# Two transformer blocks on one Trainium2 core: head norms squared before the rotation, and a new written order of work

## The reference

```
# A: cross attention            xn = layernorm(x); yn = layernorm(ctx)
q = xn @ Wq; k, v = split(yn @ Wkv); x = x + softmax(q k^T / 4) v @ Wproj + bproj
# B: MLP                        x = x + gelu(layernorm(x) @ W1 + b1) @ W2 + b2      (256 -> 1024 -> 256)
# C: cross attention with rotated, normalised heads
xn = x * rsqrt(mean(x*x) + 1e-5) * norm_w
q, k, v = xn @ wq, ctx @ wkv
q, k = rotate(q), rotate(k)     # x * cos + concat(-x2, x1) * sin in each head
q = q / max(norm(q), 1e-12); k = k / max(norm(k), 1e-12)     # per head
x = x + softmax(4 * q k^T) v @ wout
```

## Time and profile before

| | us |
|---|---|
| time, median of 3 runs | 364.57 |
| time of the profiled execution | 364.86 |
| its span, first to last instruction | 363.0 |
| TensorE busy | 350.7 |
| VectorE busy | 273.1 |
| ScalarE busy | 263.8 |
| GpSimd busy | 192.9 |

### The profile page before, as it was taken

How to read it: one execution, slowest core, us unless ns; L and a number is a source line. 1 busy time by engine, 2 the same in 40 slices (tenths; PEclk the granted TensorE clock), 3 DMA queues, 4 the chain that set the end, 5 groups by cost and what they waited for, 6 DMA issues and landing times.

```text
span 363.0 us, 11434 instructions
## 1 busy us (share of the span) xinstructions
PE 350.7 (97%) x4497; PEld 318.6 (88%) x4497; DVE 273.1 (75%) x654; ACT 263.8 (73%) x533; POOL 192.9 (53%) x194
## 2 busy tenths in 40 slices
PE   7799899999999999999999999999999999999996
PEld 7688788878878889999999999998989999988885
DVE  4869978988977985758578787687877756868742
ACT  3575676769677578849497896977988959975662
POOL 2553480875734261121974679637839476295910
PEclk9999999999999999999999999999999999999999
DMA  7940602001001000010001000001001010100000
GB/s 220 293 128 3 205 2 61 32 3 32 2 2 31 5 2 3 2 31 2 0 17 32 16 2 3 13 29 45 20 2 43 2 47 31 31 16 16 17 31 30
DMA packets 14837, 13.60 MB, mean 37 GB/s; under 512 B 1473, under 2 KB 14017, under 8 KB 14785
## 3 DMA queue, kind: packets, MB, share of 16 engines
q1 hardware_dynamic: 14640, 12.87, 11.5%
q10 hardware_dynamic: 144, 0.01, 0.0%
HBM read 10.78 MB, written 2.10 MB: 35 GB/s over the span
## 4 chain that ended last, share of the span: by engine, by line
PE 51%; POOL 5%; issue 2%; DVE 2%; ACT 2%; POOLq 2%; ACTq 0%; DVEq 0%
PE banks_s L1257 11%; PE bank_o L1269 7%; PE bank_y L1269 6%; PE bank_qk L1096 5%; POOL norm_inv L403 4%; PE bank_y L1323 3%; PE banks_s L1312 3%; PE bank_qk L1102 2%; PE bank_t L1102 2%; POOLq L65 1%; PE bank_o L1303 1%; PE bank_y L1330 1%; PE bank_t L1210 1%; PE bank_y L1096 1%; PE banks_s L1175 1%
## 5 line engine op out<-in xcount | busy, mean ns | idle before, releaser
L403 POOL TENSOR_TENSOR norm_inv<-norm_sq_min,minus_half 128x32 f32<-128x32 f32 x16 | 88.0, 5502 | 25.7 <-DVE norm_sq_min L2388 25.7
L357 POOL TENSOR_TENSOR masked<-qkT_r,cols 128x512 fp32r<-128x512 f32 x32 | 32.6, 1039 | 40.8 <-issue 21.9
L2296 DVE TENSOR_REDUCE row_max<-banks_s 128x8 f32<-128x1024 f32 x32 | 37.6, 1217 | 2.4 <-PE banks_s L1175 2.2
L617 ACT ACTIVATE PT<-banks_s 128x1024 f32<-128x1024 f32 x32 | 31.1, 1023 | 6.2 <-PE banks_s L1199 6.1
L1257 PE MATMUL banks_s<-lnT_hi,W_hi 128*128 128x256 f32 x120 | 35.4, 295 | 0.0
L717 ACT ACTIVATE PT<-banks_s 128x1024 f32<-128x1024 f32 x32 | 31.5, 1022 | 4.6 <-PE banks_s L1312 4.6
L1257 PE MATMUL banks_s<-lnT_hi,W_lo 128*128 128x256 f32 x120 | 33.9, 282 | 0.0
L1257 PE MATMUL banks_s<-lnT_lo,W_hi 128*128 128x256 f32 x120 | 33.8, 282 | 0.0
L1175 PE MATMUL banks_s<-masked,qkT_r 32*128 32x256 f32 x768 | 31.5, 293 | 2.2 <-DVE row_max L2296 1.0
L1175 PEld LDWEIGHTS banks_s<-masked,qkT_r 32*128 32x128 f32 x768 | 25.0, 183 | 8.2 <-issue 3.5
L396 POOL TENSOR_TENSOR cT_r<-ctx_in,cT_r 128x256 fp32r<-128x256 f32 x16 | 11.7, 738 | 36.7 <-ACT cT_r L687 36.7
(11 more groups left out here) (193 smaller groups left out, 1074.8 us busy)
## 6 DMA issues: line engine op xcount, KB each, us to landing
x_all<-in_x SPq DMA_DIRECT2D x16, 128.0 KB, 3.3
ctx_in<-in_ctx SPq DMA_DIRECT2D x16, 128.0 KB, 4.5
W_s<-in_L_xattn_W SPq DMA_DIRECT2D x2, 1024.0 KB, 8.3
ctx_in<-in_ctx_T SPq DMA_DIRECT2D x16, 128.0 KB, 2.2
out<-x_all SPq DMA_DIRECT2D x16, 128.0 KB, 2.0
Wkv_s<-in_L_xattn_Wkv SPq DMA_DIRECT2D x1, 512.0 KB, 5.1
Wkv_s<-in_L_xattn_wkv SPq DMA_DIRECT2D x1, 512.0 KB, 5.5
Wq_s<-in_L_xattn_Wq SPq DMA_DIRECT2D x1, 256.0 KB, 4.3
```

Of the source, the lines that this page charges most:

```text
L357: nc.gpsimd.tensor_tensor(masked[:, r, 1, :, half, :], qkT_r[:, t % AHEAD, 1, :, :].bitcast(fp32), ones, ALU.mult)\
L403: nc.gpsimd.tensor_tensor(norm_inv[:, j, :], norm_sq_min[:, j, :], minus_half[:, :], ALU.pow).then_inc(c_norm_inv, 1)
L617: nc.scalar.activation(PT[:, 2 * h:2 * h + 2, :], banks_s[:, 2 * h:2 * h + 2, :], ACT.Exp, scale=HD ** -0.5)\
L2296: v.tensor_reduce(row_max[:, 8 * h:8 * h + 8], banks_s[:, 2 * h:2 * h + 2, :].rearrange("p n (r k) -> p (n r) k", k=TOK), AX.X, ALU.max).t ...
```

## The change

The functions of block C (semaphore c_rot_sq becomes c_sq, buffer rot_sq becomes head_sq):

```diff
+POWERS = 16
+HALF_EXPONENT = 1597463007.0
...
             def squares(t):
-                act.wait_ge(c_rot, t + 1)
+                act.wait_ge(C["qk_mm"], t + 1)
+                if t == 0:
+                    act.wait_ge(w2_lo_done, 4)
                 wait(act, c_norm_sq, t)
-                nc.scalar.activation(rot_sq[:, :], rot[:, t % 2, :], ACT.Square).then_inc(c_rot_sq, 1)
+                nc.scalar.activation(head_sq[:, :], bank_qk[:, :], ACT.Square).then_inc(c_sq, 1)
...
             def turns(t):
-                dve.wait_ge(C["qk_mm"], t + 1)
+                dve.wait_ge(c_sq, t + 1)
...
             def square_sums(t):
-                dve.wait_ge(c_rot_sq, t + 1)
+                dve.wait_ge(c_sq, t + 1)
...
-                wait(dve, c_norm_inv, t - 1)
+                wait(dve, c_norm_inv, min(t - 1, POWERS))
...
+            def head_norms_root(t):
+                j, done = t % 2, 9 * (t - POWERS)
+                norm, root = norm_sq_min[:, j, :], norm_inv[:, j, :]
+                dve.wait_ge(c_norm_min, 2 * t + 2)
+                dve.wait_ge(c_unit, t - 1)
+                v.tensor_scalar(root.bitcast(int32), norm.bitcast(int32), -0.5, HALF_EXPONENT, ALU.mult, ALU.add).then_inc(c_root, 1)
+                for n in range(3):
...
             def units(t):
-                dve.wait_ge(c_norm_inv, t + 1)
+                if t < POWERS:
+                    dve.wait_ge(c_norm_inv, t + 1)
+                else:
+                    dve.wait_ge(c_norm_root, t - POWERS + 1)
+                dve.wait_ge(c_rot, t + 1)
```

The lists of all engines are written anew. Apart from fillers and waits they hold the same calls. Fillers go from 151 transposes in 20 calls to 111 in 14. The head of TensorE's list:

```diff
-            busy(11, bank_t)
+            query_bias_mm()
             inputs_a(0)
-            query_bias_mm()
             key_value_bias_mm()
+            busy(9, bank_qk)
```

The first MLP pair starts sooner among the calls of block A: turn_b(0) before shifted_a(10), up_b(0, 0) before scores_a(13), down_b(0, ...) before scores_a(14) and scores_a(15). ScalarE's list changes between Exp and Gelu 18 times, against 16 before. SyncE's list:

```diff
             load_c(7)
+            store(0)
             load_c(8)
+            store(1)
             load_c(9)
-            store(0)
-            store(1)
             store(2)
```

More of the change, by code:

```diff
@@ new lines, in _ @@
+            pe.wait_ge(c_rope, 2)
+            maxima_a(15)
+            down_b(1, 0, range(3, 4))
+            pe.wait_ge(b_lnT_lo, 3)
+            weighted_a(14)
+            pe.wait_ge(a_exped[0], 15)
+            pe.wait_ge(a_exped[1], 15)
+            shifted_a(15)
+            pe.wait_ge(a_maxT, 16)
+            keys_c(1)
+            pe.wait_ge(A["oT_ready"], 15)
+            inputs_c(2)
+            queries_c(1)
+            pe.wait_ge(A["res_ready"], 14)
+            down_b(1, 1, range(4))
@@ L1826, in _ @@
             queries_c(4)
-            up_b(3, 3, bank_s[3])
             pe.wait_ge(c_inT_lo, 5)
             inputs_c(5)
+            pe.wait_ge(b_x, 6)
+            back_c(0)
+            pe.wait_ge(c_exped[1], 2)
+            up_b(3, 2, bank_s[2])
+            pe.wait_ge(c_unit_lo, 3)
+            normed_c(0)
+            pe.wait_ge(C["on_ready"], 1)
+            weighted_c(1)
+            pe.wait_ge(c_inT_lo, 6)
+            values_c(3)
+            up_b(3, 3, bank_s[3])
+            pe.wait_ge(C["oT_ready"], 2)
+            back_c(1)
+            pe.wait_ge(c_onT_lo, 1)
+            units_T(3)
             pe.wait_ge(c_rope, 10)
-            project_c(0)
-            pe.wait_ge(c_onT_lo, 1)
-            normed_c(1)
+            keys_c(5)
             pe.wait_ge(b_gelu, 13)
@@ L1893, in _ @@
             scores_c(4)
[L1894 removed]
+            pe.wait_ge(C["oT_ready"], 4)
+            back_c(3)
+            pe.wait_ge(C["v_ready"], 6)
+            turn_b(5)
+            pe.wait_ge(c_onT_lo, 3)
             down_b(4, 0, range(0, 3))
+            pe.wait_ge(C["res_ready"], 2)
+            keys_c(7)
             down_b(4, 0, range(3, 4))
             pe.wait_ge(C["on_ready"], 4)
[L1898 removed]
+            weighted_c(4)
             pe.wait_ge(b_x, 9)
[L1900 to L1908 removed]
+            units_T(6)
+            pe.wait_ge(b_lnT_lo, 6)
+            inputs_c(8)
+            queries_c(7)
             pe.wait_ge(c_exped[0], 5)
@@ L1911, in _ @@
             scores_c(5)
-            pe.wait_ge(C["res_ready"], 4)
-            keys_c(7)
             pe.wait_ge(C["oT_ready"], 5)
-            back_c(4)
-            queries_c(7)
-            pe.wait_ge(c_unit_lo, 6)
-            units_T(6)
-            pe.wait_ge(b_lnT_lo, 6)
-            values_c(7)
-            pe.wait_ge(C["on_ready"], 5)
-            weighted_c(5)
+            down_b(4, 1, range(4))
             pe.wait_ge(c_exped[0], 6)
@@ L2060, in _ @@
             down_b(7, 0, range(0, 3))
+            pe.wait_ge(c_rope, 26)
+            keys_c(13)
+            queries_c(13)
             down_b(7, 0, range(3, 4))
-            pe.wait_ge(c_rope, 26)
-            project_c(9)
+            pe.wait_ge(C["on_ready"], 10)
+            weighted_c(10)
+            pe.wait_ge(C["v_ready"], 12)
+            values_c(12)
             pe.wait_ge(b_x, 15)
             units_T(11)
-            pe.wait_ge(c_inT_lo, 14)
-            values_c(12)
-            pe.wait_ge(C["on_ready"], 10)
-            weighted_c(10)
+            pe.wait_ge(C["oT_ready"], 11)
+            down_b(7, 1, range(4))
+            pe.wait_ge(c_rope, 28)
+            project_c(9)
+            pe.wait_ge(c_unit_lo, 12)
+            units_T(12)
+            pe.wait_ge(b_x, 16)
+            back_c(10)
             pe.wait_ge(C["res_ready"], 10)
-            keys_c(13)
-            queries_c(13)
+            keys_c(14)
+            pe.wait_ge(C["v_ready"], 13)
+            inputs_c(14)
             pe.wait_ge(c_exped[0], 11)
```

1803 lines of the change are left out of this document (884 added, 919 removed).

## The result

The changed kernel takes 369.97 us (median of 4 runs, 368.13 to 370.88) against 364.58 for the kernel before on the same chip: ratio 1.0136, 95% interval 1.0094 to 1.0178. It is slower, by 5.4 us. The prediction was 358.3 us, with 0.15 for slower. The profiled execution is the fastest of the four: 368.13 us, span 366.2.

What follows compares the result with a forecast made beforehand. TensorE, busy 350.7 of 363.0 us, was taken as the bound. Span 325.6 + 15.4 + 15.2 = 356.2, plus 0.5 for table loads and 1.86 around the span, made 358.6, less 0.29 for the median: 358.3 us, range 356.5 to 360.

Steps and rivals of the forecast that it cites:

- Other moves: Mainly first attention: earlier MLP pair 0, two more table loads +0.5 us, store and load order 0, GpSimd order 0.
- the sign that I had set for being wrong: One of three signs against the forecast: TensorE idle for more than 4 us in the first attention.
- If the 8.2 us of early waits stay: Head and first attention: TensorE's waits up to queries_c(14) stay 8.2 us, so that call starts at 324.84 us.
- Fillers, -4.36: TensorE's filler transposes go from 151 to 111, 40 at 0.109 us each: -4.36 us, bounds 0 and -4.36.
- The tail: After queries_c(14): 15.4 us to units_T(15) where the trace had 18.0, then 15.2 us to the end, unchanged.
- The middle: From 140 to 320 us TensorE lacks only 0.45 us of full; it should stay within 0.5 us.
- The squares: Squares read bank_qk ahead of the rotation: 2.0 us off the chain to the power, price elsewhere taken as 0.
- the rival's mechanism: Slower case: late squares on ScalarE hold bank_qk and TensorE waits; 367.2 us at a lateness of 2.5 us; chance 0.15.
- the cover of 3.14 us and more: TensorE calls between queries_c and its next bank_qk call, at least 3.14 us against 2.15 needed, covering ScalarE 1.0 us late.
- given back in the first attention: Rival: tiles 11 to 15 queue behind gelu calls and table loads, costing 5.1 us: 363.4 us; chance 0.10.
- The clock rival: Rival: TensorE idles in the head, 4.4 to about 6.0 us, and the clock halves until 11 us: +3.1, 361.4; chance 0.05.

Runs made afterwards that it cites:

- b1_early_weights: The kernel before with four VectorE calls, three w1_split and queries_weight(), pulled ahead to the changed kernel's places: 373.75 us, ratio 1.0255.
- e1: e1_late_qweight: the changed kernel with VectorE's queries_weight() moved back behind maxima_split(15): 367.98 us, ratio 1.0097 to the kernel before.
- e3: The changed kernel with queries_weight() and w1_split(1), (2), (3) moved back in VectorE's list: 368.81 us, ratio 1.0111 to the kernel before.
- e7: e3 with statistics(9), (11) and (12) also moved later in VectorE's list: 370.02 us, ratio 1.0151 to the kernel before.
- g188b: Old order for calls begun before 188 us, then the changed kernel's order, with 16 fillers fewer in the tail: 362.05 us, ratio 0.9915.
- g188c: g188b with 10 more fillers removed behind project_c(12): 361.98 us, ratio 0.9923 to the kernel before.
- g284: Old order for calls begun before 284 us on all engines but SyncE's, then the changed kernel's order: 364.57 us, ratio 0.9996.
- e4: The kernel before with only the squares changed, read from bank_qk ahead of turns, in the old lists: 370.05 us, ratio 1.0140.
- e6_late_w2: The changed kernel with GpSimd's W2 splits moved behind masked_lo(6) and inverse_std(13): 369.67 us, ratio 1.0142 to the kernel before.

## Why the prediction was wrong

**Failed step: "Other moves", the first attention taken as 0 and +0.5.** I weighed the MLP pair, the table loads, the stores and GpSimd there, each by its own rows, and never the order of VectorE's list: four weight calls, statistics and norms ahead of the row maxima. That VectorE was busy for 100.5 of 120 us in that stretch was in the earlier trace rows, and I used the number beside it, ScalarE's 85.3. Measured: 6.9 us more TensorE idleness there and 3.3 us of half clock, 10.2 us where I had 0.5; the sign that I had set for being wrong, more than 4 us idle there, came. b1_early_weights shows that such a move alone, in the old order, costs 8.9 us. That it is what the new order loses by is not shown: putting that work back gave 2.0, 1.2 and 0 us (e1, e3, e7), and nothing where executions of an equal clock can be compared, and with the loads, the W2 splits or TensorE's spacing mended as well the waits moved on. What is shown is that the calls of before 188 us carry the loss. Which of them do is open: no part that was tried carries it alone, and no run put back the whole list of one engine for the first attention. Of TensorE's 9.9 us of waits 1.6 were for ScalarE and 0.9 for GpSimd.

**"If the 8.2 us of early waits stay": they did not.** queries_c(14) starts at 333.20, not 324.84. These 8.4 us are most of the miss; the tail adds 1.4.

**Fillers, -4.36: right in count** (111 of L1355). The price of 0.109 us each holds only where nothing else sets the pace: in the tail 26 fewer gave 0.3 us at most (g188b, g188c), and g284 with 16 fewer than before gained nothing, with waits at its seam. What the 27 ahead of queries_c(14) are worth no run shows by itself.

**The tail: half right.** From the record's end of queries_c(14) to units_T(15) 15.9 us, against 17.9 before read the same way (the prediction had 15.4 for 18.0): the shorter chain works as described. units of tile 15 came 14.6 us behind it, forecast about 14; that GpSimd came 1.1 us late to the first power is a part of the difference. From units_T(15) to the end 16.2 us, not 15.2, and all of that 1.0 us lies between units_T(15) and scores_c(15), 4.65 us for 3.64: the new order has weighted_c(14) waiting for its exponents, behind a project and 18 fillers. So of 2.6 us forecast in the tail 1.0 came.

**The middle: right.** 0.37 us lacking. **The squares: right for this order, and the rival's mechanism is real.** e4 prices it at 5.2 us where the order gives no cover; in the new one VectorE waited 2.6 us in all, and TensorE in the second attention never for bank_qk. That the cover of 3.14 us and more, which I counted along the list, is what kept TensorE free agrees with this; no run took it away in the new order.

**The rival "given back in the first attention" had the place, not the cause.** It put the loss at tiles 11 to 15, behind gelu calls; it came from 40 us on, at tiles 1 to 8, mostly behind VectorE, and was twice as large. **The clock rival** had the mechanism and the wrong place: nothing fell in the head, where TensorE idled for 1.0 us behind the warming transposes; it fell at 70.1 us, 2.1 us into a wait of 2.5.

**The clock.** Executions of one kernel differ by it: e1_late_qweight took 367.1 to 367.5 us at 0.995, 368.4 at 0.991, 371.9 at 0.981 and 373.8 at 0.977; from the first to the last that is 6.5 us, and (1 - clock) x span makes 6.7. The changed kernel had 0.991 once and 0.986 three times, which is 3.3 and 5.1 us of its span; the kernel before had 1.00 in 52 of the 61 executions beside the experiments, and about 0.995 in nine, which took some 1.5 us longer. In time, then, the clock makes 5.1 of the median's 5.4 us. The 6.9 us of new idleness are offset by the 40 fillers (4.4 us) and by 2.2 us that I can place by no row. The Trainium skill ("TensorE: Matmul & The Clock Gate", A second HAM failure mode: psum-queue depth-cycling) describes a matmul kernel in which TensorE idles shortly and often between groups of matmuls, so that its clock goes back and forth between the half and the full rate. The trace agrees in part: the half rate came with no stop longer than 2.5 us, in a stretch where TensorE was busy for 17.45 of 20. But it came once, and not behind the stops of 0.84 to 1.47 us between 39 and 55 us, nor behind the one of 1.60 us at 93 us.

## What to carry to other kernels

Where a second engine is nearly as busy as the first (here VectorE, 100.5 of 120 us), read its list too: in b1_early_weights 6.8 us of its work, pulled ahead of calls that TensorE waits for, came back as 6.5 us of waits and 3.3 of half clock. When a new order of everything is judged, compare for every engine what it has done at the same TensorE call; here VectorE and GpSimd were 8 and 9 us ahead by my estimate, which the lists and the old trace's durations would have given before any run. When undoing one part at a time, compare executions at the same granted clock: the 2.0 us of e1_late_qweight are gone by that measure. And a change that costs 5.2 us in the old order and, as far as the rows show, nothing in the one made for it (the squares) should be judged in its own order.

## What the hardware showed

A VectorE tensor_scalar from SBUF to SBUF, 128x256, took 1426 ns while GpSimd split W2, and 346 to 348 with GpSimd elsewhere: e6_late_w2 moved only the GpSimd calls. The Trainium skill ("SBUF — State Buffer", Who interferes with whom) says that a tensor_scalar can run in a mode that takes a port pair shared with GpSimd, and that whoever issues first holds the pair for its whole instruction while the other waits. The trace agrees in the size: the two ran from 64.10 to 65.57 and 66.24 to 67.63 us, GpSimd's products of W2_lo beside them from 64.13 to 65.42 and 66.00 to 67.47, so each ended about 0.15 us behind the product. Of who issued first it shows little. The second product started 0.24 us ahead of VectorE's instruction; at 64.10 us the product before (62.89 to 64.18) was still under way, and the next one started 0.03 us behind VectorE.
